# Projecting one chunk of rows at a time, and storing and loading the first head group's parts in halves of their own

## The reference

```python
x = x + L0_xattn(layernorm(x), ctx, ...)
# in it: 16 heads of 16 features, causal
q = einsum('bsd,hde->bhse', x, Wq1);  k = einsum('btd,hde->bhte', x, Wk1)
v = einsum('btd,hde->bhte', x, Wv1) + bv1
scores = einsum('bhse,bhte->bhst', q, k) * 16 ** -0.5   # causal mask
o = einsum('bhst,bhte->bhse', softmax(scores), v)
```

## Time and profile before

| | us |
|---|---|
| median of 3 runs (lowest, highest) | 1379.08 (1377.55, 1393.95) |
| profiled execution, its own time | 1377.67 |
| its span, first to last instruction | 1375.9 |
| PE busy in the span | 1206.2 (88%) |
| DVE, ACT, POOL busy | 849.1, 562.1, 312.1 |
| mean granted clock of TensorE | 0.937 |

### The profile page before, as it was taken

The page is one execution under the profiler, slowest core; times in us unless marked ns, Lnnn a source line. Parts: engine busy times, 40 slices in busy tenths (PEclk is TensorE's granted clock), DMA queues, the critical chain, the costliest instruction groups (busy, mean ns, idle before and its releaser), DMA issues. The chain is left out here.

```text
span 1375.9 us, 19970 instructions
## 1 busy us (share of the span) xinstructions
PE 1206.2 (88%) x7150; PEld 847.5 (62%) x7150; DVE 849.1 (62%) x1814; ACT 562.1 (41%) x1201; POOL 312.1 (23%) x490
## 2 busy tenths in 40 slices
PE   7988999887887787999888876999999788899999
PEld 3543333332333335677667765899977667788898
DVE  4577776766555384566567786666644455865555
ACT  5215666555564355455225533210013333543332
POOL 5012222222220035544117652000010110600000
PEclk8999999999997899999979977999989999899999
DMA  5840363330441802000002000000030000000000
GB/s 192 184 116 2 55 61 48 47 48 1 71 71 43 145 7 58 1 1 1 1 20 103 2 0 1 1 1 1 1 123 0 0 1 0 1 0 16 16 17 16
DMA packets 37969, 50.71 MB, mean 37 GB/s; under 512 B 11098, under 2 KB 28784, under 8 KB 37232
## 3 DMA queue, kind: packets, MB, share of 16 engines
q1 hardware_dynamic: 37872, 49.44, 17.3%
HBM read 37.26 MB, written 11.77 MB: 36 GB/s over the span
## 5 line engine op out<-in xcount | busy, mean ns | idle before, releaser
L532 PE MATMUL PS<-ARENA 128*17 128x512 f32 (+14 forms) x2208 | 401.9, 419 | 67.1 <-ACT ARENA L1367 17.1
L532 PEld LDWEIGHTS PS<-ARENA 128*17 128x17 f32 (+5 forms) x2208 | 163.0, 127 | 239.0 <-issue 110.3
L1282 ACT ACTIVATE ARENA<-PS 128x512 f32<-128x512 f32 (+3 forms) x384 | 172.9, 490 | 143.8 <-PE PS L532 141.1
L1671 DVE TENSOR_REDUCE ARENA<-PS 128x1 f32<-128x128 f32 (+7 forms) x256 | 181.4, 751 | 66.1 <-PE PS L532 64.9
L532 PE MATMUL PS<-WQKVP,TRR 128*128 128x384 f32 x512 | 134.3, 344 | 1.5 <-ACT BC L1218 1.0
L2119 POOL TENSOR_SCALAR_AFFINE_SELECT ARENA<-ARENA 128x128 f32<-128x128 f32 x256 | 74.0, 296 | 219.0 <-ACT ARENA L1282 216.3
L532 PEld LDWEIGHTS PS<-W2P,INT 128*128 128x128 f32 x768 | 94.9, 188 | 2.8
L532 PE MATMUL PS<-W2P,INT 128*128 128x256 f32 x768 | 95.5, 279 | 0.0
L532 PEld LDWEIGHTS PS<-WQKVP,TRR 128*128 128x128 f32 x512 | 93.4, 192 | 2.6 <-ACT BC L1218 1.9
L1963 DVE SCALAR_TENSOR_TENSOR ARENA<-PS,rw,ARENA 128x384 f32<-128x384 f32 x112 | 69.2, 618 | 40.2 <-PE PS L532 39.5
L2091 POOL TENSOR_TENSOR rstd<-var,halves 128x4 f32<-128x4 f32 x36 | 38.1, 1058 | 245.8 <-DVE var L1516 197.7
(11 more groups left out here) (221 smaller groups left out, 1955.6 us busy)
## 6 DMA issues: line engine op xcount, KB each, us to landing
ARENA<-qk_parts SPq DMA_DIRECT2D x96, 128.0 KB, 5.6
qk_parts<-ARENA SPq DMA_DIRECT2D x8, 768.0 KB, 3.3
ARENA<-xq_parts SPq DMA_DIRECT2D x48, 128.0 KB, 6.0
ARENA<-in_w SPq DMA_DIRECT2D x2, 2048.0 KB, 10.7
xq_parts<-ARENA SPq DMA_DIRECT2D x8, 384.0 KB, 2.3
ARENA<-in_wqkv SPq DMA_DIRECT2D x1, 3072.0 KB, 10.0
X<-in_x SPq DMA_DIRECT2D x4, 512.0 KB, 7.1
ARENA<-in_wf SPq DMA_DIRECT2D x2, 1024.0 KB, 6.2
```

What stands on the lines that cost most here:

```text
L532: return nc.tensor.matmul(o, lhsT, rhs, start=start, stop=stop, **kw)
L1282: ins = nc.scalar.activation(PROB[GRP * (step % 2) + j][:, 0:w], PS[:, uses[key][0], 0:w], ACT.Exp, scale=HD ** -0.5)
L1671: ins = v.tensor_reduce(negm[:, n % 2, TPB * j + st:TPB * j + st + 1], PS[:, bank:bank + 2, :].rearrange("p b s -> p (b s)")[:, 0:P * (st ...
```

## The change

Four things change. (1) The order of the eight query and key projections: before, step = 4g + 2w + c; now step = 4g + 2c + w, so both projections of chunk 0 come before those of chunk 1. (2) Chunk 1 is transposed at step 1 instead of together with chunk 0, on PE and on ACT; PE waits for ACT's copies of chunk 0 at step 0 and for those of chunk 1 at step 2. At the very start ACT copies chunk 0 out before it normalizes tiles 4 to 7. (3) SP stores only the 64 feature rows of head group 0 (query, then key) first, loads pack 0 from them (query half, then key half, each behind its own store), and then stores the other 64 rows and everything else; pack 1 is loaded once the second halves have landed. (4) Eight warming matmuls instead of 36 in front of the first maxima. Waits on `parts_out` follow: stores 0 and 1 now count to 32.

```diff
+def projection(step):
+
+    g, at = divmod(step, 4)
+    return g, at % 2, at // 2
...
@@ PE, project @@
-                if step == 0:
-                    for c in (2 * b, 2 * b + 1):
-                        turn("t_in", "in", H, c, ((0, 1), (4, 5))[b], 14 if c == 0 else 0)
-                    for c in (2 * b, 2 * b + 1):
-                        turned("t_in", c)
+                if step < 2:
+                    turn("t_in", "in", H, 2 * b + step, ((0, 1), (4, 5))[b], 14 if (b, step) == (0, 0) else 0)
+                if step in (0, 2):
+                    turned("t_in", 2 * b + step // 2)
                 if step < 8:
-                    g, w, c = step // 4, step // 2 % 2, step % 2
+                    g, w, c = projection(step)
...
@@ PE, first maximum of group 0 @@
-                            busy(36, 0)
+                            busy(8, 0)
                         pe.wait_ge(pack_in[slot], 12 * 16 * (n // SLOTS + 1))
...
@@ SP @@
+            def load_half_pack(n, w):
+
+                b, h0 = n // 4, GRP * (n % 4)
+                packs, order = ((PACKQ, QPART), (PACKK, KPART))[w]
+                src = scratch[b, w].rearrange("(h e) c s -> c e h s", h=HEADS)
+                for r, part in enumerate(order):
+                    sp.dma_start(packs[n % SLOTS][HD * r:HD * r + HD, :, :],
+                                 src[part, :, h0:h0 + GRP, :]).then_inc(pack_in[n % SLOTS], 16)
...
-            for u in range(8):
-                b, g, w = u // 4, u // 2 % 2, u % 2
-                sp.wait_ge(parts_ready, 2 * (u + 1))
-                sp.dma_start(scratch[b, w, P * g:P * g + P, :, :], PARTS[u % 4]).then_inc(parts_out[u], 16)
-                if u == 1:
-                    for v in (0, 1):
-                        sp.wait_ge(parts_out[v], 16)
-                    load_pack(0)
-                    load_pack(1)
+            def load_pack(n):
+                for w in range(2):
+                    load_half_pack(n, w)
+
+            def store_parts(b, g, w, lo=0, hi=P):
+
+                sp.wait_ge(parts_ready, 8 * b + 4 * g + w + 3)
+                sp.dma_start(scratch[b, w, P * g + lo:P * g + hi, :, :], PARTS[2 * g + w][lo:hi]).then_inc(parts_out[4 * b + 2 * g + w], 16)
+
+            for w in range(2):
+                store_parts(0, 0, w, 0, GRP * HD)
+            for w in range(2):
+                sp.wait_ge(parts_out[w], 16)
+                load_half_pack(0, w)
+            for w in range(2):
+                store_parts(0, 0, w, GRP * HD, P)
+            for w in range(2):
+                store_parts(0, 1, w)
+            for w in range(2):
+                sp.wait_ge(parts_out[w], 32)
+            load_pack(1)
+            for u in range(4):
+                store_parts(1, u // 2, u % 2)
...
@@ ACT, project @@
-                if step == 0:
-                    for c in (2 * b, 2 * b + 1):
-                        evacuate("t_in", c)
+                if step < 2 and (b, step) != (0, 0):
+                    evacuate("t_in", 2 * b + step)
                 if step < 8:
-                    u = 8 * b + step
-                    key = ("qk", b, step // 4, step // 2 % 2, step % 2)
+                    g, w, c = projection(step)
+                    key = ("qk", b, g, w, c)
                     arrived(act, key)
-                    if u >= 8:
-                        act.wait_ge(parts_out[u // 2 - 4], 16)
+                    if b == 1 and c == 0:
+                        act.wait_ge(parts_out[2 * g + w], (16, 32)[g == 0])
...
             normalize("in", 0)
+            evacuate("t_in", 0)
             normalize("in", 1)
...
@@ DVE, output of group 0 @@
-                            dve.wait_ge(parts_out[k], 16)
+                            dve.wait_ge(parts_out[k], 16 if k > 1 else 32)
```

More of the change, by code:

```diff
@@ L1061, in _ @@
                      a[name].rearrange("(o e) -> o e", o=1).broadcast_to([P, EXPERTS]))
-            def load_pack(n):
[L1064 to L1069, removed]
-            for u in range(8):
-                b, g, w = u // 4, u // 2 % 2, u % 2
-                sp.wait_ge(parts_ready, 2 * (u + 1))
-                sp.dma_start(scratch[b, w, P * g:P * g + P, :, :], PARTS[u % 4]).then_inc(parts_out[u], 16)
-                if u == 1:
-                    for v in (0, 1):
-                        sp.wait_ge(parts_out[v], 16)
-                    load_pack(0)
-                    load_pack(1)
+            def load_half_pack(n, w):
[5 more added lines that the diff above has]
+                                 src[part, :, h0:h0 + GRP, :]).then_inc(pack_in[n % SLOTS], 16)
+            def load_pack(n):
+                for w in range(2):
[17 more added lines that the diff above has]
+                store_parts(1, u // 2, u % 2)
             for v in range(2, 8):
@@ L1556, in project @@
                         dve.wait_ge(parts_ready, u - 2)
-                    released(v.tensor_tensor(REST[u % 3], PS[:, uses[key][0], :], PARTS[u // 2 % 4][:, 0, 512 * (u % 2):512 * (u % 2) + 512],
+                    released(v.tensor_tensor(REST[u % 3], PS[:, uses[key][0], :], PARTS[2 * g + w][:, 0, 512 * c:512 * c + 512],
                                              ALU.subtract), key)
@@ L1560, in project @@
                     t = 8 * b + step - 1
-                    part = PARTS[t // 2 % 4]
+                    g, w, c = projection(step - 1)
+                    part = PARTS[2 * g + w]
                     dve.wait_ge(mid_ready, t + 1)
-                    drained(dve, ("qk", b, (step - 1) // 4, (step - 1) // 2 % 2, (step - 1) % 2))
-                    v.tensor_tensor(part[:, 2, 512 * (t % 2):512 * (t % 2) + 512], REST[t % 3],
-                                    part[:, 1, 512 * (t % 2):512 * (t % 2) + 512], ALU.subtract).then_inc(parts_ready, 1)
+                    drained(dve, ("qk", b, g, w, c))
+                    v.tensor_tensor(part[:, 2, 512 * c:512 * c + 512], REST[t % 3],
+                                    part[:, 1, 512 * c:512 * c + 512], ALU.subtract).then_inc(parts_ready, 1)
                 if step > 8:
```

9 lines of the change are left out of this document (4 added, 5 removed).

## The result

| | before | after |
|---|---|---|
| median of 20 executions, us | 1380.14 | 1371.35 |
| lowest, highest | 1368.51, 1393.95 | 1362.13, 1384.91 |
| profiled execution, span, us | 1375.9 | 1380.9 |
| its mean granted clock | 0.937 | 0.932 |

The ratio of after to before is 0.9945, 95% interval 0.9922 to 0.9968: 7.6 us faster, between 4.4 and 10.8. 1370 was forecast. The ratio leaves out executions more than 1.5% above the fastest of their kernel (here three of before and two of after), the medians take all of them. Executions of one kernel scatter over some 25 us, and the profiled execution of after is a long one of its kind, 5.0 us longer than the one of before. So the two traces can't be compared by their spans.

What follows compares the result with a forecast made beforehand. PE, busy 88%, was taken to bound the whole, and the chain to pack 0's landing the first stage; 5.2 + 3.4 - 0.6 + 0.3 = 8.3 us off gave 1369.4 and 1370.8, stated as 1370, range 1364 to 1377.

Steps and rivals of the forecast that it cites:

- the first rival: Clock falls in PE's gap before pack 0 lands, slowing the second batch's first two projections 3.6 us; 1373 us, chance 0.25.
- the one that I called likeliest: The forecast case: 8.3 us gained, 1370 us, with the clock kept in the gap before the first maxima; chance 0.50.
- (a): First stage: projecting chunk 0 first starts ACT's first middle part earlier; gain 4.6 to 6.0 us, 5.2 taken, half-clock side.
- (b): Stores to pack 0's loads: query loads follow the issue of the key half's store; gain 3.4 us, at worst 2.7.
- (c): Loads of pack 0: the key half's store travels beside the first ones; cost 0 to 2.4 us, 0.6 taken.
- (d): Second batch: chunk 2's projection no longer waits for chunk 3's four tiles; gain 0.3 us, from 0 to 1.
- (e): Before the first maxima: eight warmers end about 40.8, loads at 42.2; gap 1.4 us too short for a clock fall, cost nothing.
- (f): SP's second halves, whole stores and pack 1 are issued later yet land before they are needed; cost nothing, cover 25 us.
- the front doesn't move: Rival: something else holds ACT's first middle part at 25.5; only 2.8 to 3.1 us gained, 1376 us, chance 0.11.
- Half clock through the second batch: Rival: clock falls in the gap and PE never earns it back in the batch; 9 us slower, 1387 us, chance 0.04.
- Less company for the loads: Rival: pack 0's loads gain 3 us more without pack 1 behind them; gain about 12 us, 1366 us, chance 0.10.
- the last sign: Sign: the shift at the first scores (99.73, 8 us earlier) must be found again at the end, else the prediction is wrong.

Runs made afterwards that it cites:

- the repeat: The changed kernel unchanged, run once more: ratio to before 0.9991 (0.9955 to 1.0027), median 1372.36 us against 1377.35.
- e3: The changed kernel with 36 warming matmuls instead of 8: median 1370.07 us, ratio to before 0.9932 (0.9900 to 0.9965).
- e4_again: Second, timed run of the changed kernel with whole stores, pack 0 loaded first and alone, 36 warming matmuls: median 1367.16 us, ratio to before 0.9893.
- e2: Kernel before's projection order with the changed kernel's half stores and later pack 1, 24 warming matmuls: 1375.82 us in a single execution.
- e4: The changed kernel with whole stores instead of halves, pack 0 still loaded first and alone, 36 warming matmuls: profiled span 1370.2 us.
- e5: The changed kernel with 36 warming matmuls, SP holding second halves and later stores until pack 0 has landed: profiled span 1361.0 us.
- e1: New projection order alone, with before's whole stores and loads, 42 warming matmuls: 1357.30 us in a single execution; its timed repeat median 1374.35 us, ratio 0.9983.
- e6: The changed kernel with ACT's normalizations of tiles 8 to 15 moved behind steps 4 and 5, 22 warming matmuls: median 1364.68 us, ratio to before 0.9881.

## Why the prediction was right, by its steps

The forecast was 8.3 us off and 1370 us; the median fell by 8.8, to 1371.35, and the ratio gives 7.6. The number was right, but the mechanism only in part, and the closeness owes something to luck. By the prediction's own signs it would be wrong if the clock dropped between 38 and 45, and it dropped at 42.4 (40.3 in the repeat): in the first stage the case that came true is the first rival, not the one that I called likeliest. In the traces the parts add up so: 5.64 + 3.02 - 1.23 = 7.43 us at the first maximum, then 0.46 gained (from e3) and 3.8 lost, 4.1 us ahead at the second subtraction (4.8 in the repeat), and that is what stands at 81 us, about half of the 8.3. No run shows the 8.3 us themselves; that the median of the twenty fell by twice what the front shows has no cause that these runs show and may be scatter: the repeat's ratio gives 1.2 us, between 6 faster and 4 slower.

- (a) *Chunk 0 first*: 5.2 us forecast, 5.64 measured (19.86 for 25.50), and kept to the fourth low part (28.21 for 33.85). The bounds held. The side I took did not: I chose half clock because chunk 1's transposes stand between the projections, and the clock stayed at 1.00. That it isn't 6.0 is DVE's doing, whose normalizations ended at 19.21 instead of 18.75. One execution, e4_again, shows the half-clock side: it had lost the clock by its window from 17, and its first middle part started at 20.95, 4.55 us earlier than before's. The rule that I leaned on (the Trainium skill, "TensorE: Matmul & The Clock Gate", Part 4, on transposes) is neither shown nor refuted by that: with chunk 1's transposes between the projections the clock was kept in eight of the nine executions that have the new order.
- (b) *Half stores*: 3.4 us, at worst 2.7; measured 3.83 - 0.81 = 3.02. The mechanism (the loads don't wait for the landing of the key store) is right, and e2 and e4 show it; but in after it wasn't the key store's issue either that released them: the query half, issued at 25.47, landed at 29.00, and the first load went out at 29.02. The reason by halves is wrong: a half takes 3.5 us in every trace, not the 2.3 of another half-size store, which is spread over 128 partitions. The rule of the Trainium skill ("DMA: Bandwidth & Descriptors", rules for kernel authors) against splitting in disjoint partition halves held: whole stores do as well.
- (c) *The loads*: 0.6 us of cost, from 0 to 2.4; measured 14.04 - 12.81 = 1.23. The term was taken at half its size. Its mechanism is right: the key half's store ahead lands the first load 1.4 us later (4.3 for 2.9), and the bound of 2.4 held. The stores queued behind cost nothing that can be seen (e5: 14.19 without them, 14.04 and 14.39 with them).
- (d) *The second batch*: 0.3 us, from 0 to 1; where the clock is kept, e3 gives 7.50 ahead at the second subtraction against 7.04 at the first maximum, 0.46. e1, its repeat and e5 give 0.4 to 0.5 as well.
- (e) *Eight warming matmuls*: this step failed. I had them cost nothing, as PE would be done at 40.8 with a gap of 1.4 us. PE was done at 37.04, since the first stage ran at full clock, and the gap was 6.03 us. It cost 3.4 us against e3 in the trace of after and 2.7 in its repeat (3.8 and 2.6, counted from each one's first maximum); the rival had put 3.6 on it, though for two projection steps at half clock, where it was one. (The rival's 37.4 doesn't follow from its terms: 36 and 1.8 for the warmers are 37.8, a gap of 3.7 us instead of 4.1.) The rival's total, 5.5, compares with 4.1 and 4.8 in front; its time of 1373 is nearly as close to the measured one as the forecast, and the measurement can't choose between them.
- (f) *Moved work on SP*: no wait for a second half's landing appears on ACT; right.

Of the other rivals, "the front doesn't move" is refuted by 19.86. Half clock through the second batch didn't come: the clock returned at 52.6. "Less company for the loads" went the other way. Of the last sign, a shift that is found again at the end, the traces show this: at the first scores it is 5.1 us in after, 4.3 in its repeat and 7.5 in e3, but by the spans' end after is 5.0 us behind before and its repeat 7.0 ahead. Stretches of half clock outweigh it in single traces; that it carries to the end on the mean is what the first comparison of twenty executions suggests and the repeat leaves open.

## What to carry to other kernels

Warming matmuls in front of a wait are sized to the wait: when a change moves both ends of the gap (here PE's end by 6.9 us and the DMA's by 7.4), count them anew from the trace, as 28 taken out cost about three of the seven microseconds won. Too many cost as well: in e4_again 36 of them held PE 1.2 us beyond the landing of the pack. To shorten a store and reload through memory, issue the loads of a part as soon as that part has landed, without waiting for the next part's store; splitting the store in partition halves gives nothing. And when one chain has been shortened, look in it for work of the same engine that isn't of it: two normalizations moved by a few instructions brought the first maximum 3.1 us forward, against 7.4 of the whole change.

## What the hardware showed that I hadn't expected

A store of 64 partitions took longer (3.5 us, in every trace that has it) than one of 128 with twice the bytes (3.2). The loads of one pack, the same twelve DMAs, took from 12.8 to 14.9 us from the first issue to the last landing in eleven executions (before 12.8, e1 13.4 and 14.9, e6 13.5, the others 14.0 to 14.6); 1.4 us of that is a store in flight ahead of them, the rest has no cause that these runs show. And the clock: after the end of the warmers (37.0 and 37.1) it fell at 42.4 in one trace of the changed kernel and within the 41st microsecond in the other, and stretches of 17 to 27 us at half clock, with PE 0.81 to 0.95 busy in them, come in some executions and not in others, in the kernel before too. They go with the time: of the twenty executions of after, the two fastest (1362.13 and 1362.74 us) have a mean clock of 0.947 and 0.952, the two slowest (1384.91 and 1382.59) 0.928 and 0.932. That scatter is larger than the change.
